# One-core conv/attention/LSTM/expert kernel: a route stage with stationary gate weights, and the local attention's set-up moved into the first convolution stage

## The reference, cut to what matters

```
sc = softplus(scale_p)                    # 64 values
q = (relu(xw @ wq.T) + 1e-06) / sc
k = (relu(xw @ wk.T + pos) + 1e-06) / sc  # then powers, norms, heads, a 5x5 convolution of v
```

```
logits = x @ gate_w + gate_b              # 8192 tokens, 16 experts
probs = softmax(logits)
top_probs, top_idx = top_k(probs, 2);  top_probs /= sum(top_probs)
dispatch = sum(one_hot(top_idx) * top_probs)
out = sum over experts of (silu(x @ w1) * (x @ w2)) @ w3 * dispatch
```

## Time and profile before

| | us |
|---|---|
| median of 3 runs | 1367.01 |
| the profiled execution | 1367.41 |
| its span, first to last instruction | 1365.6 |
| outside the span | 1.8 |

### The profile page before, as it was taken

The page is one execution under the profiler, slowest core; times in us unless marked ns, Lnnn a source line. Parts: engine busy times, 40 slices in busy tenths (PEclk is TensorE's granted clock), DMA queues, the critical chain, the costliest instruction groups (busy, mean ns, idle before and its releaser), DMA issues. The chain is left out here.

```text
span 1365.6 us, 27455 instructions
## 1 busy us (share of the span) xinstructions
PE 1045.2 (77%) x9710; PEld 611.4 (45%) x9710; DVE 848.6 (62%) x2482; ACT 519.7 (38%) x1338; POOL 264.8 (19%) x375
## 2 busy tenths in 40 slices
PE   6778786767988756666666666666973899999996
PEld 2356652253666535454454545453542333333332
DVE  6586845745556365555555555554346688888885
ACT  3443442453443323232323232223641545554452
POOL 3303012300000000000000000000100255555555
PEclk9898997868999865555555555557985999999998
DMA  6000002000000000000000000000000775555650
GB/s 226 1 1 1 1 2 78 0 1 1 1 0 0 1 1 0 0 0 0 0 0 0 0 0 0 0 0 1 0 1 8 146 149 130 123 123 121 131 117 23
DMA packets 23059, 47.41 MB, mean 35 GB/s; under 512 B 1616, under 2 KB 5840, under 8 KB 22608
## 3 DMA queue, kind: packets, MB, share of 16 engines
q1 hardware_dynamic: 22992, 46.51, 14.7%
HBM read 43.88 MB, written 2.62 MB: 34 GB/s over the span
## 5 line engine op out<-in xcount | busy, mean ns | idle before, releaser
L1613 PE MATMUL wide<-ls_h,ls_v 128*128 128x16 f16 x2304 | 104.1, 176 | 144.4 <-DVE ls_h L1712 141.2
L2115 ACT ACTIVATE ex_gated<-wide,unscale 128x1024 f32<-128x1024 f32 x128 | 142.1, 1113 | 138.8 <-PE wide L2081 138.7
L2131 DVE TENSOR_TENSOR ex_hid<-wide,ex_gated 128x1024 f32<-128x1024 f32 x128 | 156.0, 1223 | 44.5 <-ACT ex_gated L2115 40.0
L1613 PEld LDWEIGHTS wide<-ls_h,ls_v 128*128 128x128 bf16 x2304 | 81.0, 105 | 213.4 <-DVE ls_h L1712 213.4
L2057 POOL TENSOR_TENSOR ex_acc<-ex_part,ex_acc 128x512 f32<-128x512 f32 x120 | 152.3, 1270 | 94.9 <-DVE ex_part L2147 80.7
L1702 DVE TENSOR_TENSOR_SCAN ls_cells<-ls_terms 128x48 f32<-128x48 f32 x256 | 73.6, 288 | 124.1 <-ACT ls_terms L1637 124.1
L1637 ACT ACTIVATE ls_terms<-wide 128x32 f32<-128x32 f32 x256 | 54.4, 213 | 229.6 <-PE wide L1618 229.6
L2093 PE MATMUL wide<-ex_hid,w 128*64 128x512 f32 x512 | 116.7, 598 | 0.0
L2081 PE MATMUL wide<-xh,wh 64*128 64x512 f16 x512 | 98.8, 382 | 4.6 <-PEq L81 3.2
L2081 PE MATMUL wide<-xh,wl 64*128 64x512 f16 x512 | 98.0, 379 | 0.0
L2081 PE MATMUL wide<-xl,wh 64*128 64x512 f16 x512 | 97.8, 378 | 0.0
(11 more groups left out here) (364 smaller groups left out, 1925.4 us busy)
## 6 DMA issues: line engine op xcount, KB each, us to landing
ex_d<-route SPq DMA_DIRECT2D x64, 512.0 KB, 7.9
par_attn<-in_attn SPq DMA_DIRECT2D x1, 2704.0 KB, 13.3
par_rest<-in_rest SPq DMA_DIRECT2D x1, 2539.0 KB, 18.6
L_xin<-in_x SPq DMA_DIRECT2D x8, 256.0 KB, 5.6
w<-in_w SPq DMA_DIRECT2D x1, 2048.0 KB, 7.9
out<-ex_acc SPq DMA_DIRECT2D x16, 128.0 KB, 4.6
w<-in_w SPq DMA_DIRECT2D x1, 512.0 KB, 8.9
route<-ro_dt SPq DMA_DIRECT2D x8, 64.0 KB, 1.7
```

Of the source, the lines that this page charges most:

```text
L1613: pe.matmul(ig[:, g, :] if g < 2 else o, vp[part][:, g, :], h1[:], start=False, stop=False, skip_group_check=True)
L2115: act.activation(gated[:, n % 2, :], pair_of_up(n // GS, 2 * (n % GS))[:], ACT.Silu, scale=m.unscale[:, 0:1]).then_inc(s["gated_ready"], 1)
L2131: dve.tensor_tensor(hid[:, n % (2 * GS), :], pair_of_up(n // GS, 2 * (n % GS) + 1)[:], gated[:, n % 2, :], ALU.mult).then_inc(s["hid_ready ...
```

## The change

**In the first convolution stage.** POOL zeroes `xw` behind its last copy into the padded input, and behind each of its first four adds (tiles 0 to 3) it waits for that add and copies four windows into `xw`: the 16 copies of the first four window groups. ACT leaves its loop one pair early: the third pair's end is written out, and the four steps of softplus stand between `hidden(2)` and `ffn_out(2)`. DVE does its nine set-up instructions behind the last convolution. The buffers that hold these results are now allocated around both stages.

**In the attention stage.** What is left of the set-up are the padding's norms, which `qkv` doesn't read. PE no longer waits for the set-up ahead of `qkv(0)`, and POOL only raises the count for 16 copies.

**In the route stage.** The gate weights are stationary. Each of 8 matmuls streams the 512 tokens of a tile through 32 columns of weights, and four tiles write to four groups of 32 partitions of one PSUM bank. ACT adds the bias to the first bank and DVE to the second (the bias is now one value for each partition). 8 transposes of 128 x 128 bring the tokens to the partitions in PSUM, where DVE reads them. The DVE chain is two full-width instructions shorter and one is fused away. The normalised weights `en` are computed on POOL, beside DVE's search for the second expert, and DVE's last instruction keeps `en` where an expert was chosen. 8 transposes of 128 x 128 go back, ACT and DVE copy one bank each, and two DMAs of 256 KB store them. The scratch tensor has the tile as its outermost dimension.

The diff, cut to its core:

```diff
@@ conv_ffn_stage, POOL
+                pool.memset(a_xw[:], 0.0).then_inc(xw_zeroed, 1)
             for t in range(TILES):
                 pool.wait_ge(branch_ready, t + 3)
                 y = tile_of(out, t)
                 pool.tensor_tensor(y, branch[:, t % 2, :], y, ALU.add).then_inc(out_ready, 1)
+                if layer == 0 and t < 4:
+                    pool.wait_ge(xw_zeroed, 1)
+                    pool.wait_ge(out_ready, t + 3)
+                    for f in range(4):
+                        pool.tensor_copy(slots(a_xw[:, 4 * t + f, :], 0, 7, 7),
+                                         square_of(out, t, 7 * (f // 2), 7 * (f % 2), 7, 7)).then_inc(xw_filled, 1)
@@ conv_ffn_stage, ACT
-            with act.Fori(0, PAIRS - 1) as i:
+            with act.Fori(0, PAIRS - 2) as i:
                 first_tap(i + 1)
                 hidden(i)
                 ffn_out(i)
+            first_tap(PAIRS - 1)
+            hidden(PAIRS - 2)
+            if layer == 0:
+                scale_parts()        # Abs, Exp, Ln, Relu on p["scale"], as before in the attention stage
+            ffn_out(PAIRS - 2)
@@ conv_ffn_stage, DVE
+            if layer == 0:
+                dve.wait_ge(m.attn_landed, 16)
+                dve.wait_ge(scale_ready, 4)
+                step(dve.tensor_tensor(a_inv_sc[:], a_sc[:, 2, :], a_sc[:, 3, :], ALU.add))
...
+                step(dve.scalar_tensor_tensor(a_pad[:, 0, :], a_pos[:, 0, :], 0.0, a_floor[:], ALU.max, ALU.add))
             finish(PAIRS - 1)
@@ attention_stage
-            pool.memset(xw[:], 0.0).then_inc(s["zeroed"], 1)
-            for G in range(6):
-                gather(G)
+            pool.sem_inc(s["xw_ready"], pieces_before(4))
+            gather(4)
+            gather(5)
...
-            pe.wait_ge(s["setup"], 8)
-            pe.wait_ge(s["act_setup"], 5)
             qkv(0)
             qkv(1)
+            pe.wait_ge(s["act_setup"], 1)
@@ route_stage, PE
+            for b in range(2):
+                for k in range(QT):
+                    mm = pe.matmul(bank[4 + b][2 * E * k:2 * E * (k + 1), :], p["gate_w"], tile_of(m.xn, QT * b + k),
+                                   start=True, stop=True)
+                mm.then_inc(s["gate_done"], 1)
+            for b in range(2):
+                pe.wait_ge(s["lgt1_ready" if b else "lgt0_ready"], 1)
+                for q in range(4):
+                    mm = pe.transpose(bank[6 + b][:, q * P:(q + 1) * P], lgt[:, b, q * P:(q + 1) * P], p["ident"])
+                mm.then_inc(s["lg_done"], 1)
@@ route_stage, POOL
+            pool.wait_ge(s["e_ready"], 1)
+            pool.wait_ge(s["scale_ready"], 1)
+            pool.tensor_tensor(en[:], e[:], over(top[:, 3, :]), ALU.mult).then_inc(s["en_ready"], 1)
@@ route_stage, DVE
+            dve.tensor_scalar(lgt[:, 1, :], bank[5][:], p["gate_b"][:, 0:1], None, ALU.add).then_inc(s["lgt1_ready"], 1)
...
-            link(dve.tensor_scalar(pick[:], lg[:], 0.0, None, ALU.is_equal))
-            link(dve.tensor_tensor(pick[:], pick[:], idx, ALU.mult))
+            link(dve.scalar_tensor_tensor(pick[:], lg[:], 0.0, idx, ALU.is_equal, ALU.mult))
...
-            link(dve.tensor_tensor(pick[:], masks[:, 0], masks[:, 1], ALU.add))
-            link(dve.tensor_tensor(e2[:], pick[:], e[:], ALU.mult))
-            link(dve.tensor_reduce(top[:, 3, :], e2[:], AXX, ALU.add))
-            link(dve.reciprocal(top[:, 0, :], top[:, 3, :]))
-            dve.tensor_tensor(e2[:], e2[:], over(top[:, 0, :]), ALU.mult).then_inc(s["d_ready"], 1)
+            link(dve.scalar_tensor_tensor(e2[:], mask[:], -2.0, e2[:], ALU.mult, ALU.add))
+            dve.wait_ge(s["en_ready"], 1)
+            dve.scalar_tensor_tensor(d[:], e2[:], 0.0, en[:], ALU.is_lt, ALU.mult).then_inc(s["d_ready"], 1)
+            dve.wait_ge(s["dt_done"], 2)
+            dve.tensor_copy(dt[:, 1, :], bank[5][:]).then_inc(s["dt1_ready"], 1)
```

More of the change, by code:

```diff
@@ L1926, in _ @@
             act.wait_ge(s["exp_in"], 1)
             act.activation(e[:], lg[:], ACT.Exp).then_inc(s["e_ready"], 1)
-            for t in range(TILES):
-                act.wait_ge(s["dt_done"], t + 1)
-                act.activation(dt[:, t, :], bank[6 + t % 2][0:2 * E, :], ACT.Copy).then_inc(s["dt_ready"], 1)
+            act.wait_ge(s["dt_done"], 1)
+            act.activation(dt[:, 0, :], bank[4][:], ACT.Copy).then_inc(s["dt0_ready"], 1)
         @block.sync
         def _(sp):
-            for t in range(TILES):
-                sp.wait_ge(s["dt_ready"], t + 1)
-                sp.dma_start(m.route[:, :, t, :].rearrange("h e n -> (h e) n"), dt[:, t, :])\
+            for b in range(2):
+                sp.wait_ge(s["dt1_ready" if b else "dt0_ready"], 1)
+                sp.dma_start(m.route[QT * b:QT * (b + 1)].rearrange("t h e n -> (t h e) n"), dt[:, b, :])\
@@ L1937, in _, with over @@
                   .then_inc(s["stored"], 16)
[L1938 removed]
+            sp.wait_ge(s["stored"], 32)
+        def over(v):
+            return v.unsqueeze(2).broadcast_to([P, G, E])
+        @block.gpsimd
+        def _(pool):
+            pool.wait_ge(s["e_ready"], 1)
+            pool.wait_ge(s["scale_ready"], 1)
+            pool.tensor_tensor(en[:], e[:], over(top[:, 3, :]), ALU.mult).then_inc(s["en_ready"], 1)
         @block.vector
         def _(dve):
[L1942 to L1948 removed]
@@ L2364, in lay_out @@
     q["gate_w"] = both(v["L3_ffn_gate_w"])
[L2365 removed]
+    q["gate_b"] = np.tile(v["L3_ffn_gate_b"], 8)[:, None]
     q["idx_w"] = rows(np.tile(np.arange(E, 0, -1), 2).astype(f))
```

162 lines of the change are left out of this document (80 added, 82 removed).

## The result

| | before | after |
|---|---|---|
| median of five runs, us | 1366.92 | 1347.13 |
| lowest and highest, us | 1358.62 to 1367.26 | 1337.93 to 1348.22 |
| ratio, with 95% interval | | 0.9846 [0.9822, 0.9871] |

A forecast was written before the change was run, and what follows sets the result against it. From 1062.18 us on, mostly PE's expert-stage products bound the kernel; ahead, whatever ends last in each stage. Terms of -12.2 in and behind the route stage and -2.0 at the front gave -14.2, so 1352.8 us; range 1347.5 to 1358.

The forecast's parts named there:

- route, logits: Route stage: eight side-by-side gate matmuls end in 3.8 us, DVE's chain starts at 1023.4 instead of 1032.60; -9.2 us.
- route, DVE's chain: Route stage: fewer DVE instructions save 3.0 us, POOL's product for `en` holds DVE for 2.4; -0.6 us.
- route, the way back: Route stage's end: transposes, copy and store take 6.3 us instead of 9.4, with 1.0 for the larger DMA; -3.1 us.
- expert stage: Expert stage's opening: PE may start at the lower clock, 1.3 us more at half clock; +0.7 us.
- attention, opening: Attention stage's opening: PE no longer waits for set-up, first product at 57.2 instead of 62.54; -5.3 us.
- first convolution stage: First convolution stage: POOL's adds and window copies slow DVE's streams by 1.6 and 1.7 us; +3.3 us.
- attention, behind its opening: Attention stage after its opening: no change was priced there; 0 us.
- The serial rival: Route stage: gate matmuls run one after another, 5.0 us later, 1357.8 us in all; chance 0.08.
- the 5 that I had named as a warning: Expert stage: a granted clock of 0.5 for more than 5 us would show the forecast wrong.
- The rival in which the clock stays down for 28 us and more: Expert stage: lower clock cancels the gain from 28 us on; with 40 us, 1372.8 us; chance 0.02.
- the rival in which POOL hardly blocks DVE: Convolution and route stages: POOL's work fits between DVE's steps, -2.4 and -2.8 us more, 1347.6 us; chance 0.15.
- The DMAs' part: Expert stage: the scratch tensor's layout makes loads contiguous, but they are hidden behind the first up products; 0 us.

The follow-up runs named there:

- route_only: The changed kernel's new route stage with the old convolution and attention front of the kernel before; 1352.97 us, ratio 0.9902 to before.
- en_on_dve: The changed kernel with the product for `en` on DVE, right behind the reciprocal, instead of on POOL; 1342.27 us, ratio 0.9819 to before.
- warm_experts: The changed kernel with three unread 512-column matmuls ahead of the route stage's last transposes and three behind them; 1344.58 us, ratio 0.9841 to before.
- warm_front: The changed kernel with three unread 512-column matmuls behind the first convolution stage's last product; 1346.68 us, ratio 0.9853 to before.
- copies_tripled: The changed kernel with eight more unread small window copies on POOL behind the four after each of the first four adds; 1351.53 us, ratio 0.9892 to before.
- front_only: The changed kernel's new convolution and attention set-up with the old route stage; 1361.02 us, ratio 0.9959 to before.
- copies_in_gap: The changed kernel with window copies of tiles 0-1 moved behind tile 5's add, tiles 2-3 to the attention stage's opening; 1346.63 us, ratio 0.9854 to before.
- copy_wide: The changed kernel with one more unread 512-column POOL copy behind the four small ones of each of the first four adds; 1348.51 us, ratio 0.986 to before.
- combined_warm: combined plus two unread matmuls behind the first convolution stage's last product; 1342.0 us, ratio 0.9801 to before.
- before_again: The kernel before once more, with no edit, for a second trace; 1366.73 us in a single run.
- combined: The changed kernel with copies_in_gap, en_on_dve and four unread matmuls ahead of and behind the route's last transposes; 1344.01 us, ratio 0.9818 to before.

## Why the prediction was right or wrong

The terms, measured between the traces of before and after (the typical one):

| term | forecast | measured |
|---|---|---|
| route, logits | -9.2 | -9.6 |
| route, DVE's chain | -0.6 | -1.6 |
| route, the way back | -3.1 | -3.7 |
| expert stage | +0.7 | +1.0 |
| attention, opening | -5.3 | -4.7 |
| first convolution stage | +3.3 | +1.5 |
| attention, behind its opening | 0 | -2.6 |
| all other stages | 0 | +0.1 |
| sum | -14.2 | -19.6 |

**Logits: right.** The eight matmuls end after 3.64 us (3.8 forecast) at a granted clock of 0.50, so four of them do run side by side. The serial rival would have ended them after 8.8 and is refuted; route_only shows the same 3.64.

**DVE's chain: mechanism right, price too high.** One step beside POOL's product did grow, to 2.83. But POOL holds DVE for 1.6, not for 2.4. POOL's product takes 2.71 from 1027.01, and 0.92 of this lie beside DVE's step before (L2012, to 1027.93); it ends 1.79 behind that step, and the next one takes 1.60 longer. en_on_dve confirms the 1.6 with a step of 1.23 at the same place. The forecast doubled the time of POOL's adds and got 2.4; only the 1.79 behind DVE's step could hold it.

**Way back: right.** DVE's copy ends 2.75 behind the last step (2.7 forecast), and the expert stage starts 2.98 later, where it was 2.6 behind ACT's last copy before. So the four times larger store costs 0.4, not 1.0.

**Expert stage: right in kind.** It opens at half clock for 5.5 us instead of 3.5, longer than the 5 that I had named as a warning, and is 1.0 us longer (304.4 against 303.4; 0.7 forecast). warm_experts shows that it is the clock: with the products in between, the stage opens at 1.00 and the loss is gone. The rival in which the clock stays down for 28 us and more is refuted.

**Attention, opening: nearly right.** L481 starts 0.4 us after the stage's first instruction, as said. The products ran at the lower level until 64 us, as feared, and the opening gained 4.7 of 5.3. In warm_front, and in two kernels without its edit, the opening ran at the higher level.

**First convolution stage: the step that failed.** It is the sentence "I give a small copy 0.15, between nothing and its 0.23. Per pair: 1.27 + 6 x 0.15 = 2.2, less what is lost now: 1.6 and 1.7." Measured are 8.04 - 7.55 = 0.5 and 8.07 - 7.36 = 0.7; another 0.3 was there before these two streams, from the first one (8.94 here, 8.67 in the other trace of after, 8.47 before). The runs put in its place: about 1.0 for an add that lies wholly in a stream, about 0.01 for a small copy. I had only the price of a copy five times as large (0.39) and took a value between nothing and the small copy's own length. The cost doesn't go by the length: what POOL does in the first 0.12 us or so behind a DVE step is free (0.19 beside the product of the route stage). The undisturbed stream of ten takes 6.92, 0.69 from step to step, and POOL's copies in copies_tripled came at 0.70 each, one for each DVE step.

The Trainium skill ("SBUF — State Buffer", Who interferes with whom) has DVE instructions with two SBUF inputs and GpSimd instructions that read SBUF exclude each other by a lock. For the order of waiting the traces agree: a POOL copy that began at 34.65 ended only 0.14 behind DVE's step, and DVE's step that began at 33.61 lasted until 35.39, 0.56 past POOL's add. The price that I drew from that rule, the copy's full length, is not what they show: 98 columns cost DVE 0.01 of 0.23, and of the 2.7 of the route stage's product DVE paid 1.6. The measurement decides the price. The same section of the Trainium skill says that a GpSimd instruction that only writes doesn't disturb such a DVE instruction. The trace of after agrees: POOL's zeroing runs from 16.31 to 18.11, and DVE's steps that start at 16.85 and 17.52 take 0.76 each, as undisturbed ones do. That the first stream varies has another source, POOL's copies of the input, which start as their DMAs land; six of its ten steps took 1.07 to 1.11 in this trace, five took 0.94 to 1.11 in that of before.

**The term that was missing.** The forecast put nothing for the attention stage behind its opening, without a reason; there the trace of after is 2.6 us shorter, in a place where the change edits nothing. It is the largest part of the miss. The kernels before and after differ there in where the clock is low.

DVE's first steps of the second, third, fifth and sixth group in the trace of after:

```profile
72.72 1.22 DVE L773 SCALAR_TENSOR_TENSOR att_base<-wide,att_floor 128x1024 f32<-128x1024 f32 x1
81.00 1.22 DVE L773 SCALAR_TENSOR_TENSOR att_base<-wide,att_floor 128x1024 f32<-128x1024 f32 x1
...
97.57 1.22 DVE L773 SCALAR_TENSOR_TENSOR att_base<-wide,att_floor 128x1024 f32<-128x1024 f32 x1
112.12 1.22 DVE L773 SCALAR_TENSOR_TENSOR att_base<-wide,att_floor 128x1024 f32<-128x1024 f32 x1
```

and in the trace of before, with the stretch in question:

```profile
75.96 1.22 DVE L750 SCALAR_TENSOR_TENSOR att_base<-wide,att_floor 128x1024 f32<-128x1024 f32 x1
85.16 1.22 DVE L750 SCALAR_TENSOR_TENSOR att_base<-wide,att_floor 128x1024 f32<-128x1024 f32 x1 [0.83 <-PE wide L445]
...
101.74 1.22 DVE L750 SCALAR_TENSOR_TENSOR att_base<-wide,att_floor 128x1024 f32<-128x1024 f32 x1
117.95 1.22 DVE L750 SCALAR_TENSOR_TENSOR att_base<-wide,att_floor 128x1024 f32<-128x1024 f32 x1
```

```profile
78.00:82.00 4.00, 4.00 (x40) 2.84 (x41) 3.67 (x4) 1.37 (x3) 0.00 (x0) 0.50 0.00 0
```

The second group takes 8.28 in after and 9.20 in before, where DVE waits 0.83 for PE's products at a clock of 0.50; the fifth group, the one with the first finish, takes 14.55 and 16.21. In the fifth group before had a clock of 0.58 and 0.56 at 104 to 106 and 106 to 108 us, and after 1.00 throughout. These two courses recur. The short one is in both traces of after, in front_only, route_only, copies_in_gap, copies_tripled, copy_wide and combined_warm; the long one in before, before_again, warm_front, warm_experts and combined (8.9 to 9.2 and about 16.2); en_on_dve has 8.28 and then 16.17. The traces of before and after show the granted clock differ; the instructions of these groups are the same. Why a kernel takes the one or the other stays open: route_only has the old attention stage and took the short course in its profiled run (1348.1 us), while four of its six runs were 1352.9 to 1355.3. en_on_dve and warm_experts have exactly the front of after, differ from it only some 950 us later, and took the long fifth group. Two traces of after itself, 1337.93 and 1347.79 us, differ by 2.0 us from the stage's first instruction to the tenth group (102.9 and 104.9), and by 6.5 more in the stages up to about 460 us. So this term is not a property of the new set-up that I could have worked out from its instructions, and part of the measured gain may be a matter of which course is likelier behind which start; that was not tested beyond one or two traces of each kernel.

Without this term the front would be -3.2, which lies between the forecast of -2.0 and the -5.6 of front_only, and the whole -17.0: 1350, inside the range. That is the size of the miss: 1.8 from the copies, 2.6 from the clock's course, 1.0 from POOL's product, 1.0 from the logits and the store, less 1.0 from the attention opening, the experts and the other stages.

The total also lies within 0.5 us of the rival in which POOL hardly blocks DVE (1347.6). That is chance: there the product for `en` costs DVE nothing and the front pays 0.5, and measured are 1.6 for the one and 1.5 for the other; the clock's 2.6 made up for it.

The DMAs' part was rightly priced at nothing. The packets of the whole kernel fall from 23059 to 10675, and the expert weights' loads (`ex_d`) land after 6.3 us at the median instead of 7.9. The stage got no shorter by it: in en_on_dve, whose opening was at the lower clock for 2.8 us, it took 303.3 us, against 303.4 before with 3.5 us of it.

## What to carry to other kernels

Price a GpSimd neighbour of a DVE stream by how far it runs past the end of a DVE step, from a row of its size: many tiny copies were nearly free for DVE and dear for POOL, one 512-column add was dear for both. Move filler work in small pieces, but see what is queued behind it on POOL. And after every change of a mixed PE and DVE loop, compare the granted clock stretch by stretch before a gain or a loss is given to an instruction: here 2.6 of 19.6 us came from a stretch that no edit touched. Compare such a stretch with every kernel that shares its code before an edit gets the credit: warm_front's full clock was there without its products.

## What the runs showed of the hardware that was not expected

- Four matmuls with 32-column weights into four groups of 32 partitions run side by side even with 512 columns of f32 each: eight in 3.64 us at half clock, where one of the ordinary kind (L481) takes 2.06 with its latency.
- A GpSimd copy of 98 columns beside a stream of two-input DVE steps of 0.69 us ends 0.14 us behind a DVE step and so comes at one each 0.70, and DVE pays 0.01; a copy of 512 columns costs DVE 0.36, an add of 512 columns about 1, a product of 1024 columns 1.6. A GpSimd zeroing of 1.8 us beside the same stream cost it nothing.
- Two stores of 256 KB in place of eight of 64 KB cost 0.4 us at the end of the stage.
- Six unread products around eight transposes brought the expert stage's opening from 0.50 to 1.00 and about 2 us, and eight did so in two more kernels (302.6 and 302.7 us against 304.4).
- The same instructions of the attention stage ran with low clocks in different places: its opening took 7.1 us at 0.56 in after and 5.0 at 1.00 in two kernels that are edited only in the route stage.
